# Attention stages of a two-layer decoder: head stacks split over the two halves of TensorE's rows, and row scores issued in turn with transposed scores

## The chip, the cores and the metric

The kernel runs on one core of a Trainium2 chip. The metric is the time of one execution on the device in microseconds (us). Three runs of the kernel before gave 5631.46, 5637.95 and 5650.88 us; the median is 5637.95.

Names: PE is TensorE (PEld its weight loads), DVE VectorE, ACT ScalarE, POOL GpSimd, SP SyncE, which issues nearly all DMAs here. An "S" in the text on the change means a matmul of row scores, "K" one of transposed scores, "sel" the one that adds the shift.

## The reference, cut to what matters

There are 64 batches of 128 tokens with 128 features, and a context of 77 tokens. Six sublayers follow each other, each with a residual and a layer norm behind it: a bidirectional selective scan with a feed-forward part, a gated and masked cross attention, a block of self attention and a mixture of experts, a self attention with normed queries and keys, a cross attention, and a quantized feed-forward part. The four attentions have 16 heads of 8 features. The plain one:

```python
q = _split_heads(query @ wq + wq_b, H)      # (B, H, 128, 8)
k = _split_heads(key_in @ wk + wk_b, H)     # (B, H, 128 or 77, 8)
v = _split_heads(value @ wv + wv_b, H)
logits = jnp.einsum('bhqd,bhkd->bhqk', q, k) / jnp.sqrt(8)
attn = jax.nn.softmax(logits, axis=-1)
out = jnp.einsum('bhqk,bhkd->bhqd', attn, v)
return out @ wo + wo_b
```

In the gated one a mask is added to the logits and `attn` is multiplied by a given array. All arithmetic is float32; the scores must have nearly that precision.

## The kernel before, in words

`build` (L2630 on) runs seven stages one after the other: the scan; the gated cross attention (tag `x0`, tiles named `x_...` in the trace); the self attention in front of the experts (`f0`, tiles `f_...`); the experts; the self attention of layer 1 (`a1`, tiles `a_...`); the cross attention of layer 1 (`x1`, tiles `x_...` again); the quantized part. Four of them are the function `attention` (L70). The text calls these x0, f, a and x1. From 2611 us x0 is running, from 3285 f, from 4255 a, from 4889 x1.

**Stacks.** Queries and keys are split into three bfloat16 parts each (high, middle, low) by DVE (L637, L642) and POOL (L824, L831). SP writes the parts to DRAM (`save_parts`, L237) and reads them back as stacks (`fill_stack`, L249): `Qs` and `Ks` have, for each head, 48 rows: six pairs of parts times 8 features, so that one bfloat16 matmul with 48 rows of contraction gives the scores of a head. The other 80 of the 128 partitions are zero (memsets L577 and L807), and the matmuls read all 128. A stack holds one group of four batches side by side in its columns, and there are two (parity of the group).

**Steps and chunks.** Work goes in steps, one batch each, of four chunks; a chunk is four heads. A group has 16 chunks. `turn` is two groups, and `Fori` repeats it. All engines run through the same sequence of steps and chunks and are tied by semaphores only. In the stages f, a and x1, which have no gate, chunk c of step b holds on PE:

- `scores` (L342): four matmuls, queries by keys, into one of two banks. DVE takes the maximum over the keys (`maximum`, L669), negated.
- `shifted` (L360), of batch b-1 (chunk c-1; the last chunk of it comes with chunk 0 of the next step): transposed scores, keys by queries, four times a matmul of `Ks` and `Qs` and one of `sel` with the turned maxima `nmT`, which adds the negated maximum. ACT takes the exponential into `pT` (L512).
- `values` (L380), of batch b-2: four float32 matmuls, each into its own 32 columns of the array.
- in chunk 0 `turn_max` (L353), the transpose of the split maxima of batch b-1, into the bank that the output projection uses too; DVE copies it to `nmT` (`maxima_rows`, L697) in its chunk 0.
- in chunk 1 `turn_out` (L395), in chunk 3 `turn_back` (L403) of batch b-3, and `out` (L407), the output projection of batch b-4, in chunk 3 (chunk 2 in cross attentions), which waits (L411) until `nmT` of batch b-1 is copied. A bias row with one row of contraction follows it (L414), except in a, which has no bias.
- `prep` (L309), the projections of a coming group, in the slots that `slot` (L95 to L101) gives.

In the gated stage x0 the exponential is taken on rows, and PE turns the weights instead (`turn_weights`, L372); there are no shifted scores.

DVE has in chunk 3 also `split_maxima` (L686, four small operations) and `add_residual` (L719), in chunk 2 `weighted` (L707), in chunk 1 `norm` (L738). SP's queue (`turn`, L271) is in order: load x, save parts, store, load gate, fill the stack, load the residual.

Of the kernel before, what the change touches and what calls it, by code (L numbers as in the profile page):

```python
# [13 lines left out]
P = 128  # L14
# [55 lines left out]
def attention(nc, const, banks, tag, x_in, x_out, wq, wk, wv, wo, scale, bq=None, bk=None, bv=None, bo=None,  # L70
# [15 lines left out]
    TAIL = 6  # L86
# [8 lines left out]
    if rms:  # L95
        slot = {"x": -8, "qt": -7, "kt": -6, "qn": -3, "kn": -2, "v": 3}
        later = {"v": 1, "high": 0, "middle": 1, "squares": 0, "root": 1, "norm": 2}
    elif ln is not None:
        slot, later = {"x": -5, "q": -4, "k": -3, "v": 3}, {"v": 3, "high": 1, "middle": 2}
    else:  # L100
        slot, later = {"x": -7, "q": -5, "c": -4, "k": -3, "v": 3}, {"v": 3, "high": 1, "middle": 2}  # L101
# [12 lines left out]
    with ExitStack() as st:  # L114
# [6 lines left out]
        dram_q = nc.dram_tensor(f"{tag}_q_parts", (2, PARTS, P, GT), BF16, kind="Internal").ap()  # L121
        dram_k = nc.dram_tensor(f"{tag}_k_parts", (2, sum(K_TIMES), P, kt), BF16, kind="Internal").ap()
# [22 lines left out]
        Qs = sb("Qs", [P, 2, H, GT], BF16)  # L145
        Ks = sb("Ks", [P, 2, H, kt], BF16)
# [18 lines left out]
        s_w = sem("weights"); s_setup = sem("setup"); s_zero = sem("zeroed"); s_xp = sem("x_loaded"); s_xr = [sem(f"residual_loaded{l}", 16) for l in range(2)]  # L165
# [3 lines left out]
        s_ps = sem("parts_stored", 16 * (PARTS + 1)); s_stk = [sem(f"stack_loaded{l}", 16 * (PARTS + 1)) for l in range(2)]  # L169
# [15 lines left out]
        NZ = 2 + (gate is None) + (sk < P)  # L185
# [6 lines left out]
        def columns(t, half, u, lo, n):  # L192

            c = 2 * half + u
            return t[:, 4 * c:4 * c + 4, u * VC + lo:u * VC + lo + n]

# [5 lines left out]
        def _(sp):  # L202
# [34 lines left out]
            def save_parts(g, par):  # L237
# [4 lines left out]
                save(dram_q[par], qp[:, 0])  # L242
                sp.wait_ge(s_lo.sem, s_lo.at(g, 2))
                at = 0
                for part, times in enumerate(K_TIMES):
                    save(dram_k[par, at:at + times], qp[:, 1, part:part + 1, 0:kt].to_broadcast([P, times, kt]))
                    at += times

            def fill_stack(g, par):  # L249
                def fill(stack_rows, parts):  # L250
                    sp.dma_start(stack_rows.rearrange("p h t -> p (h t)"),
                                 parts.rearrange("a (d h) t -> (a d) (h t)", d=DH)).then_inc(s_stk[par].sem, 16)
                sp.wait_ge(s_ps.sem, s_ps.at(g + 1))
                sp.wait_ge(s_use.sem, s_use.at((g - 1) * GB))
# [16 lines left out]
            def turn(i, first=False, last=False):  # L271
                for l in range(2):
# [3 lines left out]
                    if not (last and l):  # L276
                        save_parts(g + 1, 1 - l)
# [2437 lines left out]
```

## Time and profile before

The profiled execution took 5632.96 us, its span (first to last instruction) is 5630.9 us.

| engine | busy us of the span | share | instructions |
|---|---|---|---|
| PE | 4125.1 | 73% | 29561 |
| PE weight loads | 2373.7 | 42% | 29564 |
| DVE | 4485.0 | 80% | 8773 |
| ACT | 2780.7 | 49% | 6405 |
| POOL | 3082.7 | 55% | 3374 |

The busy time of PE counts matmuls whose ends are modelled, and matmuls that follow each other overlap; what a matmul costs in a stream is the distance of the starts. In the rows below "[0.20 <-DVE x]" is idle time of the engine ahead of the instruction and what ended it. The mean granted clock of TensorE was 0.856 of full speed over the span; it has two levels, 1.2 and 2.4 GHz. DMA moved 420.49 MB, at a mean of 75 GB/s.

### The profile page before, as it was taken

How to read it: one execution, taken by the hardware profiler on the slowest of the kernel's cores; microseconds unless marked ns; L12 is line 12 of the kernel's file. 1: busy time of each engine (PE TensorE's matmuls, PEld its weight loads, DVE VectorE, ACT ScalarE, POOL GpSimd, SP SyncE). 2: the span in 40 equal slices, each digit the busy share in tenths (PEclk: the TensorE clock that was granted, in tenths of full speed). 3: DMA queues.
4: the chain of work that ended last, by engine and by line, in shares of the span. 5: the costliest groups of instructions: out<-in, count | busy, mean ns of one | idle time of the engine just before them, and what ended most of it. 6: DMA issues, size and time to landing. Idle time of an engine off the chain costs nothing. (4 is left out here: it accounts for less than half of the span.)

```text
span 5630.9 us, 104474 instructions
## 1 busy us (share of the span) xinstructions
PE 4125.1 (73%) x29561; PEld 2373.7 (42%) x29564; DVE 4485.0 (80%) x8773; ACT 2780.7 (49%) x6405; POOL 3082.7 (55%) x3374
## 2 busy tenths in 40 slices
PE   5777777777777778775878858896374887699943
PEld 2333333333323233332555536665363665466621
DVE  5999999999999999995888867775145777666678
ACT  4555555455545555453666633444464444344434
POOL 6877777777777777874555532223543222323202
PEclk8989989989899989987888779996696888899965
DMA  2110111111110111112545436664124555466511
GB/s 81 64 65 34 66 66 66 51 50 66 66 59 39 66 66 66 55 44 53 92 79 93 74 73 109 111 108 144 53 82 95 96 96 91 78 117 109 99 38 30
DMA packets 319765, 420.49 MB, mean 75 GB/s; under 512 B 39955, under 2 KB 301286, under 8 KB 308710
## 3 DMA queue, kind: packets, MB, share of 16 engines
q1 hardware_dynamic: 315110, 408.16, 31.0%
q0 software_dynamic: 4352, 8.95, 0.4%
q8 instruction: 110, 1.80, 0.1%
q14 instruction: 193, 1.58, 0.1%
HBM read 307.46 MB, written 109.58 MB: 74 GB/s over the span
## 5 line engine op out<-in xcount | busy, mean ns | idle before, releaser
L2177 POOL TENSOR_TENSOR m_h<-m_dtu,m_Bb 128x512 f32<-128x512 f32 x1024 | 1584.2, 1578 | 240.8 <-PE bank L1812 234.9
L1812 PE MATMUL bank<-m_h,ident 128*128 128x512 f32 x2048 | 1211.8, 684 | 504.1 <-DVE m_h L2076 491.2
L1812 PEld LDWEIGHTS bank<-m_h,ident 128*128 128x128 f32 x2048 | 365.3, 207 | 1168.6 <-DVE m_h L2076 1011.0
L2070 DVE TENSOR_TENSOR_SCAN m_h<-m_dA,m_h 128x512 f32<-128x512 f32 x512 | 746.7, 1458 | 6.3 <-DVE m_sz L2003 5.9
L2076 DVE TENSOR_TENSOR m_h<-m_h,bank 128x512 f32<-128x512 f32 x1024 | 671.4, 656 | 4.9 <-DVE m_h L2070 3.7
L2070 DVE TENSOR_TENSOR_SCAN m_h<-bank,m_h 128x512 f32<-128x512 f32 x512 | 620.1, 1211 | 27.8 <-DVE m_sz L2003 11.8
L1959 ACT ACTIVATE bank<-m_dt,m_A 128x512 f32<-128x512 f32 x512 | 352.4, 688 | 494.0 <-DVE m_h L2070 436.0
L1959 ACT ACTIVATE m_dA<-m_dt,m_A 128x512 f32<-128x512 f32 x512 | 367.1, 717 | 430.4 <-DVE m_h L2070 426.6
L519 ACT ACTIVATE x_sm<-x_sm,x_nm 128x77 f32<-128x77 f32 x1024 | 353.5, 348 | 115.1 <-DVE x_nm L682 114.6
L859 POOL TENSOR_TENSOR x_sm<-x_sm,x_gp 128x308 f32<-128x308 f32 x256 | 219.3, 858 | 153.5 <-ACT x_sm L519 150.3
L377 PE MATMUL bank<-ident,x_sm 128*77 128x128 f32 x1024 | 197.7, 325 | 112.6 <-DVE x_pT L705 99.2
L684 DVE TENSOR_REDUCE f_nm<-bank 128x4 f32<-128x512 f32 x256 | 175.8, 688 | 116.0 <-PE bank L349 115.3
L874 POOL TENSOR_TENSOR x_var<-x_var,half_pow 128x1 f32<-128x1 f32 x128 | 69.7, 544 | 354.5 <-DVE x_var L736 354.5
L1756 PE MATMUL bank<-m_xTp,m_wck 128*128 128x512 f32 x512 | 253.8, 599 | 12.7 <-ACT m_xTp L1874 12.7
L512 ACT ACTIVATE f_pT<-bank 128x512 f32<-128x512 f32 x256 | 153.0, 598 | 220.3 <-PE bank L369 219.0
L512 ACT ACTIVATE x_pT<-bank 77x512 f32<-77x512 f32 x256 | 151.9, 593 | 214.6 <-PE bank L369 212.4
L512 ACT ACTIVATE a_pT<-bank 128x512 f32<-128x512 f32 x256 | 153.0, 598 | 206.7 <-PE bank L369 205.6
L391 PE MATMUL bank<-x_pT,x_vB 128*32 128x128 f32 x4096 | 234.2, 304 | 11.0 <-ACT x_ou L528 10.8
L684 DVE TENSOR_REDUCE x_nm<-bank 128x4 f32<-128x308 f32 x256 | 121.7, 476 | 128.3 <-PE bank L349 126.7
L874 POOL TENSOR_TENSOR a_var<-a_var,half_pow 128x1 f32<-128x1 f32 x64 | 34.7, 542 | 335.5 <-DVE a_var L736 335.5
L684 DVE TENSOR_REDUCE a_nm<-bank 128x4 f32<-128x512 f32 x256 | 175.1, 685 | 48.7 <-PE bank L349 46.7
L1805 PE MATMUL bank<-m_Cs,m_selC 80*128 80x512 bf16 x512 | 207.5, 405 | 0.0
(424 smaller groups left out, 10613.5 us busy)
## 6 DMA issues: line engine op xcount, KB each, us to landing
m_Bb<-m_B SPq DMA_DIRECT2D x32, 4096.0 KB, 12.0
x_Ks<-x_k_parts SPq DMA_DIRECT2D x32, 462.0 KB
x_q_parts<-x_qp SPq DMA_DIRECT2D x32, 384.0 KB, 3.8
x_Qs<-x_q_parts SPq DMA_DIRECT2D x32, 384.0 KB
f_Ks<-f_k_parts SPq DMA_DIRECT2D x16, 768.0 KB
a_Ks<-a_k_parts SPq DMA_DIRECT2D x16, 768.0 KB
x_xp<-x_stage SPq DMA_DIRECT2D x32, 256.0 KB
x_Qs<-x_q_parts SPq DMA_DIRECT2D x32, 256.0 KB
```

The source lines that it names most:

```text
L391: ins = pe.matmul(bankO[j * VT:(j + 1) * VT, half * S:(half + 1) * S], vB[:, lb % 2, 4 * c + j, :], pT[:, lb % 2, 4 * c + j, :], start=(c ...
L512: act.activation(pT[0:sk, p, 4 * c:4 * c + 4, :].rearrange("p h t -> p (h t)"), src, ACT.Exp).then_inc(s_e.sem, 1)
L519: ins = act.activation(sm[:, lm % 2, h, :], sm[:, lm % 2, h, :], ACT.Exp, bias=nm[:, lm % 2, 0, h:h + 1], accum_out=den[:, lm, h:h + 1])
L684: v.tensor_reduce(nm[:, p, 0, 4 * c:4 * c + 4], src, AX.X, ALU.max, negate=True).then_inc(s_Sf.sem, 1)
L859: pool.tensor_tensor(ws, ws, gp[:, lm // GB, lm % GB, :].unsqueeze(1).to_broadcast([P, 4, S2]), ALU.mult).then_inc(s_pg.sem, 1)
L1756: ins = pe.matmul(o, wck[:, d, part, c * P:(c + 1) * P], xTp[:, :, part:part + S], start=(part == 0), stop=(part == CK - 1))
L1805: pe.matmul(banks[2 + s % 2], selC[:, s, :], Cs[:, d, :], start=True, stop=True).then_inc(s_C.sem, 1)
L1812: pe.matmul(banks[4 + c], ident[:], h[:, k % RING, :], start=(s == 0), stop=(s == NS - 1)).then_inc(s_ya.sem, 1)
L1959: act.activation(decays[k % AHEAD], dt[:, d, c, :], ACT.Exp, scale=A[:, d, c, s:s + 1]).then_inc(s_dA.sem, 1)
L2070: v.tensor_tensor_scan(h[:, k % RING, :], decays[k % AHEAD], h[:, k % RING, :], 0.0, ALU.mult, ALU.add).then_inc(s_h.sem, 1)
L2076: v.tensor_tensor(h[:, k % RING, :], h[:, k % RING, :], banks[2 + s % 2], ALU.mult).then_inc(s_hC.sem, 1)
L2177: pool.tensor_tensor(h[:, k % RING, :], dtu[:, d, c, :], Bb[:, d, s, :], ALU.mult).then_inc(s_dB.sem, 1)
```

## The change

The stacks get half as many columns. A group's first two batches lie in partitions 0 to 47 of `Qs` and `Ks`, the other two in partitions 64 to 111. Each matmul on them reads 48 partitions (`rows(q)`), no longer 128, and the memsets of `Qs`, `Ks`, `nmT` and `pT` go, as does the semaphore for them; `values` reads only the rows that are written. `nmT` and `sel` exist for both halves (three more `affine_select` in the constants). SP saves and fills by halves: four more saves and four more fills per group, the same bytes. The first half may be filled as soon as the first two batches two groups back are used, and is queued ahead of the store.

In the stages without a gate the transposed scores move from one batch to two batches behind the row scores, so they always lie in the other half, and the two are issued in turn, head by head. `turn_max` moves from chunk 0 to chunk 1, `maxima_rows` to DVE's chunk 2. Everything from `values` on comes one batch later (`LATER`), and the tail is one step longer. The V projection moves from slot 3 to 4, and its evacuation to chunk 8 of a group (in a from chunk 4, else from 6). In the gated stage the order stays; only rows, memsets and DMAs change there, and the place of the V projection.

```diff
+    LATER = 1 if gate is None else 0
+    TAIL = 6 + LATER
+    HB = GB // 2
-        slot = {"x": -8, "qt": -7, "kt": -6, "qn": -3, "kn": -2, "v": 3}
-        later = {"v": 1, "high": 0, "middle": 1, "squares": 0, "root": 1, "norm": 2}
+        slot = {"x": -8, "qt": -7, "kt": -6, "qn": -3, "kn": -2, "v": 4}
+        later = {"v": 4, "high": 0, "middle": 1, "squares": 0, "root": 1, "norm": 2}
...
-        Qs = sb("Qs", [P, 2, H, GT], BF16)
-        Ks = sb("Ks", [P, 2, H, kt], BF16)
+        Qs = sb("Qs", [P, 2, H, HB * S], BF16)
+        Ks = sb("Ks", [P, 2, H, HB * sk], BF16)
...
+        def rows(q):
+            lo = 64 * (q // HB)
+            return slice(lo, lo + ROWS)
+
+        def cols(q, n):
+            return slice(q % HB * n, (q % HB + 1) * n)
...
-            def fill_stack(g, par):
+            def fill_stack(g, par, half):
...
-                sp.wait_ge(s_ps.sem, s_ps.at(g + 1))
-                sp.wait_ge(s_use.sem, s_use.at((g - 1) * GB))
+                if half == 0:
+                    sp.wait_ge(s_ps.sem, s_ps.at(g + 1))
+                sp.wait_ge(s_use.sem, s_use.at((g - 2) * GB + (half + 1) * HB))
+                lo = 64 * half
                 at = 0
                 for parts in K_TIMES:
-                    fill(Qs[at * DH:(at + parts) * DH, par], dram_q[par, 0:parts])
+                    fill(Qs[lo + at * DH:lo + (at + parts) * DH, par], dram_q[par, half, 0:parts])
                     at += parts
-                fill(Ks[0:ROWS, par], dram_k[par])
+                fill(Ks[lo:lo + ROWS, par], dram_k[par, half])
...
+                        load_gate(g + 1, 1 - l)
+                        fill_stack(g + 1, 1 - l, 0)
                     if not first:
                         store(g - 2, l)
                     if not (last and l):
-                        load_gate(g + 1, 1 - l)
-                        fill_stack(g + 1, 1 - l)
+                        fill_stack(g + 1, 1 - l, 1)
...
-            def scores(i, lb, c):
+            def scores(i, lb, c, now, then):
                 b, l, q = 8 * i + lb, lb // GB, lb % GB
...
+                tb = (lb - 2) % 8
+                tl, tq = tb // GB, tb % GB
+                if now:
+                    if c == 0 and q % HB == 0:
+                        stacked = s_stk[l][q // HB]
+                        pe.wait_ge(stacked.sem, stacked.at(i + 1))
+                    pe.wait_ge(s_Sf.sem, s_Sf.at(b, c + 1 - 2))
+                if then:
+                    pe.wait_ge(s_nmT.sem, s_nmT.at(b - 1))
+                    pe.wait_ge(s_e.sem, s_e.at(b - 2, c + 1 - 2))
                 for h in range(4):
                     hh = 4 * c + h
...
+                    if now:
+                        ins = pe.matmul(bankS[c % 2][:, h * sk:(h + 1) * sk], Qs[rows(q), l, hh, cols(q, S)],
+                                        Ks[rows(q), l, hh, cols(q, sk)], start=True, stop=True)
+                        if h == 3:
+                            ins.then_inc(s_S.sem, 1)
+                    if then:
+                        o = bankT[c % 2][0:sk, h * S:(h + 1) * S]
+                        pe.matmul(o, Ks[rows(tq), tl, hh, cols(tq, sk)], Qs[rows(tq), tl, hh, cols(tq, S)],
+                                  start=True, stop=False)
+                        ins = pe.matmul(o, sel[rows(tq), hh, 0:sk], nmT[rows(tq), tb % 2, :], start=False, stop=True)
+                        if h == 3:
+                            ins.then_inc(s_st.sem, 1)
...
-                pe.wait_ge(s_r.sem, s_r.at(b - 3))
+                pe.wait_ge(s_r.sem, s_r.at(b - 4))
...
-                    pe.wait_ge(s_nmT.sem, s_nmT.at(min(b + 4, B) if isinstance(b, int) else b + 4))
+                    pe.wait_ge(s_nmT.sem, s_nmT.at(min(b + 5, B) if isinstance(b, int) else b + 5))
...
-                if live(0):
-                    scores(i, lb, c)
+                scores(i, lb, c, live(0), gate is None and live(2))
...
-                elif c == 0:
-                    if live(2):
-                        shifted(b - 2, (lb - 2) % 8, 3)
-                    if live(1):
-                        turn_max(b - 1, (lb - 1) % 8)
-                elif live(1):
-                    shifted(b - 1, (lb - 1) % 8, c - 1)
-                if live(2):
-                    values(b - 2, (lb - 2) % 8, c)
...
+                elif c == 1 and live(1):
+                    turn_max(b - 1, (lb - 1) % 8)
+                n = 2 + LATER
+                if live(n):
+                    values(b - n, (lb - n) % 8, c)
...
-            dve.memset(Ks[:], 0.0).then_inc(s_zero.sem, 1)
-            if gate is None:
-                dve.memset(nmT[:], 0.0).then_inc(s_zero.sem, 1)
-            if sk < P:
-                dve.memset(pT[:], 0.0).then_inc(s_zero.sem, 1)
...
-                if c == 0 and live(1) and gate is None:
+                if c == 2 and live(1) and gate is None:
                     maxima_rows(v, ch, b - 1, (lb - 1) % 8)
```

## Rows read from the trace of the kernel before

**Rows 1.** stretches x0, f, a, x1: length; PE, PEld, DVE, ACT, POOL; clock; DMA
```profile
2690.00:3240.00 550.00, 445.66 (x4218) 301.08 (x4216) 476.63 (x1136) 374.30 (x1945) 306.44 (x550) 0.81 0.48 84
3400.00:3780.00 380.00, 338.67 (x4303) 241.55 (x4301) 275.10 (x798) 154.61 (x317) 102.57 (x245) 0.95 0.62 109
4330.00:4800.00 470.00, 379.35 (x4794) 287.49 (x4794) 343.25 (x934) 226.84 (x427) 117.22 (x304) 0.87 0.54 96
4950.00:5330.00 380.00, 355.30 (x5057) 258.90 (x5056) 255.01 (x934) 179.88 (x378) 115.84 (x322) 1.00 0.62 109
```

**Rows 2.** groups, DVE, same stretches: count | busy us, mean ns | idle, releasers
```profile
L679 DVE TENSOR_TENSOR x_sm<-bank,x_neg 128x308 f32<-128x308 f32 x222 | 104.6, 471 | 51.5 <-PE bank L349 50.4
...
L684 DVE TENSOR_REDUCE f_nm<-bank 128x4 f32<-128x512 f32 x187 | 128.6, 687 | 79.2 <-PE bank L349 78.8 <-issue 0.2
...
L684 DVE TENSOR_REDUCE a_nm<-bank 128x4 f32<-128x512 f32 x204 | 139.8, 685 | 37.4 <-PE bank L349 35.6
...
L684 DVE TENSOR_REDUCE x_nm<-bank 128x4 f32<-128x308 f32 x218 | 103.8, 476 | 99.6 <-PE bank L349 98.2
```

**Rows 3.** instructions in order of time, f, one chunk: start us, us, engine
```profile
3574.99 0.39 PE L349 MATMUL bank<-f_Ks,f_Qs 128*128 128x128 bf16 x4
...
3575.22 0.22 PE L367 MATMUL bank<-f_Qs,f_Ks 128*128 128x128 bf16 x1
...
3575.61 0.22 PE L369 MATMUL bank<-f_nmT,sel 128*128 128x128 bf16 x1
...
3575.76 0.43 PE L391 MATMUL bank<-f_pT,f_vB 128*32 128x128 f32 x8
...
3576.11 0.40 PE L349 MATMUL bank<-f_Ks,f_Qs 128*128 128x128 bf16 x4
```

**Rows 4.** in order of time, x1: projection, bias row, row scores, shifted scores
```profile
5154.27 0.49 PE L412 MATMUL bank<-x_w,x_oT 128*128 128x128 f32 x2
...
5154.69 0.48 PE L414 MATMUL bank<-x_bor,ones_row 1*128 1x128 f32 x2
...
5155.10 0.32 PE L349 MATMUL bank<-x_Ks,x_Qs 128*128 128x77 bf16 x4
...
5155.26 0.22 PE L367 MATMUL bank<-x_Qs,x_Ks 128*77 128x128 bf16 x1
```

**Rows 5.** in order of time, a: projection without bias, transpose
```profile
4515.76 0.49 PE L412 MATMUL bank<-a_w,a_oT 128*128 128x128 f32 x2
...
4516.08 0.27 PE L405 MATMUL bank<-ident,a_on 128*128 128x128 f32 x1
```

**Rows 6.** instruction groups, PE, stretches of f, a, a, x1
```profile
L357 PE MATMUL bank<-identb,f_nmp 128*48 128x128 bf16 x47 | 11.2, 239 | 13.1 <-DVE f_xr L725 13.0
...
L357 PE MATMUL bank<-identb,a_nmp 128*48 128x128 bf16 x51 | 11.9, 233 | 35.4 <-DVE a_r L729 33.0 <-DVE a_nmp L695 2.4
...
L367 PE MATMUL bank<-a_Qs,a_Ks 128*128 128x128 bf16 x808 | 127.8, 238 | 16.3 <-DVE a_nmT L700 16.3
...
L367 PE MATMUL bank<-x_Qs,x_Ks 128*77 128x128 bf16 x872 | 122.5, 221 | 20.3 <-DVE x_nmT L700 20.3
```

**Rows 7.** instruction group, DVE, x1: the copy of the maxima rows
```profile
L700 DVE COPY x_nmT<-bank 48x128 bf16<-48x128 bf16 x54 | 11.1, 206 | 0.0
```

**Rows 8.** in order of time, stage starts: f, f, f, f, x1, x1
```profile
3286.47 13.75 POOL L807 MEMSET f_Qs<- 128x16384 bf16 x1 [0.15 <-POOL f_vB L799]
...
3295.07 5.17 DVE L598 TENSOR_SCALAR f_lvar<-f_lst 128x4 f32<-128x4 f32 x1
...
3321.19 0.30 SPq L251 DMA_DIRECT2D f_Ks<-f_k_parts  x1
...
3336.08 1.01 PE L349 MATMUL bank<-f_Ks,f_Qs 128*128 128x128 bf16 x8 [8.18 <-issue]
...
4902.12 2.55 DVE L637 CAST x_qp<-x_qf 128x512 bf16<-128x512 f32 x1 [3.30 <-ACT x_qf L476]
...
4914.09 0.43 DVE L637 CAST x_qp<-x_qf 128x512 bf16<-128x512 f32 x1 [4.82 <-ACT x_qf L476]
```

More of the change, by code:

```diff
@@ L163, in attention @@
         lvar = sb("lvar", [P, 2, GB]) if ln is not None else None
-        s_w = sem("weights"); s_setup = sem("setup"); s_zero = sem("zeroed"); s_xp = sem("x_loaded"); s_xr = [sem(f"residual_loaded{l}", 16) for l in range(2)]
+        s_w = sem("weights"); s_setup = sem("setup"); s_xp = sem("x_loaded"); s_xr = [sem(f"residual_loaded{l}", 16) for l in range(2)]
         s_xpfree = sem("x_used"); s_pb = sem("proj_written", NU); s_pf = sem("proj_evacuated", NU)
@@ L168, in attention @@
         s_mid = sem("mid_ready", 2); s_lo = sem("lo_ready", 2)
-        s_ps = sem("parts_stored", 16 * (PARTS + 1)); s_stk = [sem(f"stack_loaded{l}", 16 * (PARTS + 1)) for l in range(2)]
+        s_ps = sem("parts_stored", 32 * (PARTS + 1)); s_stk = [[sem(f"stack_loaded{l}{half}", 16 * (PARTS + 1)) for half in range(2)] for l in range(2)]
         s_ln = sem("front_var", 1); s_lp = sem("front_pow", 1); s_xn = sem("front_norm", 1)
@@ L287, in _ @@
             save_parts(0, 0)
-            sp.wait_ge(s_zero.sem, NZ)
-            fill_stack(0, 0)
+            for half in range(2):
+                fill_stack(0, 0, half)
             turn(0, first=True)
@@ L358, in turn_max @@
                              identb[:]).then_inc(s_T.sem, 1)
-            def shifted(b, lb, c):
-                l, q = lb // GB, lb % GB
-                pe.wait_ge(s_nmT.sem, s_nmT.at(b + 1))
-                pe.wait_ge(s_e.sem, s_e.at(b, c + 1 - 2))
-                for h in range(4):
-                    hh = 4 * c + h
-                    o = bankT[c % 2][0:sk, h * S:(h + 1) * S]
-                    pe.matmul(o, Ks[:, l, hh, q * sk:(q + 1) * sk], Qs[:, l, hh, q * S:(q + 1) * S],
-                              start=True, stop=False)
-                    ins = pe.matmul(o, sel[:, hh, 0:sk], nmT[:, lb % 2, :], start=False, stop=True)
-                ins.then_inc(s_st.sem, 1)
             def turn_weights(b, lb, c):
@@ L455, in _ @@
                         prep(u, g, g)
-            pe.wait_ge(s_zero.sem, NZ)
             turn(0, first=True)
@@ L806, in _ @@
             pool.nop().then_inc(s_setup.sem, 1)
-            pool.memset(Qs[:], 0.0).then_inc(s_zero.sem, 1)
             def front(g):
@@ L2622, in _ @@
                                pattern=[[-1, P]], channel_multiplier=1).then_inc(s, 1)
-            for part in range(3):
-                pool.affine_select(out=sel[:], in_=sel[:], compare_op=ALU.not_equal, fill=1.0, base=-part * H,
+            for n, lo in enumerate((0, H, 2 * H, 64, 64 + H, 64 + 2 * H)):
+                pool.affine_select(out=sel[:], in_=sel[:], compare_op=ALU.not_equal, fill=1.0, base=-lo,
                                    pattern=[[-1, H], [0, P]], channel_multiplier=1).then_inc(s, 1)
-                pool.wait_ge(s, 8 + part)
+                pool.wait_ge(s, 8 + n)
     return {"ident": ident, "identb": identb, "ones_row": ones_row, "sel": sel, "half_pow": half_pow}
```

97 lines of the change are left out of this document (47 added, 50 removed).

## The prediction, made before the change was run

> **What bounds the kernel now.** I read the page first, then cut the span into stages with the view of stretches, then took the groups of instructions of DVE and PE in those stages, and last the instructions in order of time. The page's slices show the scan stage up to 2605 us (POOL and DVE full, PE behind them), which the change does not touch, then four attention stages. In the three without a gate PE is busy 89%, 81% and 93% of the time, DVE 72%, 73% and 67%; in the gated one DVE has 87% and PE 81% [rows 1]. The maxima per stage give the pace: 187 chunks in 380 us, 204 in 470, 218 in 380 and 222 in 550, so a group of 16 chunks (four batches) takes 32.5 us in the front attention (f), 36.9 in the layer-1 attention (a), 27.9 in the layer-1 cross attention (x1) and 39.6 in the gated one (x0). In the same rows DVE stands idle for PE's scores 78.8, 35.6 and 98.2 us [rows 2]. So f, a and x1 are bounded by PE's own stream, with some waits of PE for DVE in between; x0 is a loop in which DVE has the larger part. DMA has a mean share of at most 0.62 [rows 1], and the stacks are needed half a group after they are asked for.
>
> **What a chunk costs on PE.** At the 2.4 GHz level the row scores of f (4 matmuls) take 0.23 us from their start to the first shifted score, the 8 shifted ones follow at (3575.61-3575.22)/7 = 0.056 us, the first values matmul comes 0.15 us after the last of them, and the values take 0.35 us [rows 3]. So a chunk is 12 matmuls at their streaming rate, 0.67 us, and 0.45 us for the values and the way into them. With 77 columns the four row scores of x1 take 0.16 us at most, so a pair of load and matmul can go at 0.04 us or less [rows 4].
>
> **Row scores beside shifted scores.** The new order is S, K, sel, S, K, sel..., with S in one half of the rows and K and sel in the other. If a matmul of the other half can start beside the one in flight, the 8 of the shifted half set the length (8 x 0.055 = 0.44) and the four S hide, but for one start. That removes 0.20 of 0.23 us per chunk in f and a, 3.2 us per group, and 0.12 of 0.16, 1.9 us per group, in x1. Twelve pairs in 0.44 us are 0.037 us each, near what [rows 4] shows possible. No row shows two row halves at work together; the ends are 0 and 0.23 (f, a) or 0.16 (x1) per chunk. I take nearly the whole, because the values, four heads in four strips of 32 columns, do run beside each other: 8 in 0.35 us, which also holds a way in and out [rows 3].
> The Trainium skill, page "TensorE: Matmul & The Clock Gate", section "Part 3: Packing small matmuls — row/col tiling", says that matmuls in different row groups run at the same time, and that four of them gave 3.07 times the rate, not 4. By that share, 0.77, f and a would save 0.15 us a chunk and not 0.20, and the whole sum below would be some 32 us smaller. No row here shows it either way.
>
> **Changes of the tile shape.** A matmul with the bias row (one row of K) behind one of 128 rows costs more than its streaming: the output projection to the bias row is 0.42 us in x1, bias row to scores 0.41 [rows 4], while the same projection in a, followed by a 128-row transpose, gives way after 0.32 us [rows 5]. So a change of row shape costs 0.10 us. Before, the scores had the same 128 x 128 shape as transposes and projections; now they have 64 rows, and each way from a 128-row instruction to scores is such a change. The values and the transpose of the maxima (48 columns) already were changes on both sides. Per group: f has the output transposes and the turned-back output in each batch (8) and two projections alone in a chunk (2): 10, so 0.95 us. a: 8 and 4, 1.15 us. x1: 8 and 2, 0.95 us (the bias row at chunk 2 was one already). x0: 10 of these and one per chunk from scores to the turned weights, 26, 2.5 us of PE time. Ends: 0, if 64 against 128 rows is no change of shape, and 0.15 each, the largest way seen into another shape [rows 3].
> The Trainium skill, "TensorEngine Tiling (Array Packing)", section "Key Properties", states that changing the mode, not just the tile, drains the engine. The trace agrees where it can be seen (0.42 against 0.32 us). Without this cost the sum would be some 58 us better.
>
> **Waits that go and come.** The maxima are transposed one chunk later and needed a batch later. PE waited before that transpose 13.1 us in f (11.7 groups) and 35.4 in a (12.75 groups), and for the maxima rows 16.3 in a and 20.3 in x1 (13.6 groups) [rows 6]. That is 1.1, 4.05 and 1.5 us per group. These are moments in which DVE is behind; PE may run only two score banks ahead of it, so part comes back as a wait for a free bank. I take half in f (0.55) and a (2.0), 1.2 in x1; ends 0 and all.
> New: the output projection must wait until the maxima rows of the batch before have left their shared bank, and DVE now copies them in chunk 2, not 0. In f and a the projection stands in chunk 3, one chunk behind, and is covered. In x1 it stands in chunk 2 itself: from the start of the fused scores, 0.33 us to the last S, 0.22 for it to end [rows 6], 0.04, then DVE's maximum 0.476 [rows 2] and the copy 0.206 [rows 7], with steps 1.38 us in all; PE is there after 0.55 + 0.35 = 0.90. So 0.48 us per batch, 1.9 per group, with the scores of chunk 3 queued behind. Ends: 0 if PE is late anyway, 1 us a batch if DVE is.
> In a the V projection is now evacuated in DVE's chunk 8, the very chunk in which PE wants the bank for the next x: a maximum of 0.685 [rows 2] and a copy of as many columns from the same kind of bank, so as long, 0.22 us for S to end and some 0.2 of steps, against 0.11 + 0.45 us that PE has left, make 1.2 us per group. In f and x1 x comes later and has cover.
> x0: PE's 2.5 us per group are partly spent while it waits for DVE anyway. DVE waits for scores in 50.4 of 550 us, 9% [rows 2]. I take a quarter, 0.6 us; ends 0 and 2.5.
>
> **DMAs.** SP issues 8 instead of 4 saves and 8 instead of 4 stack loads per group, same bytes; the issue of one fill takes 0.30 us [rows 8], so some 3 us more in a queue that waits for most of a 28 to 40 us period. The first half is asked for as soon as the parts are stored, the second up to three chunks later than now, and needed two batches later. The store behind the first half has its work done later by a batch too. Nothing; if the cover failed, a late stack would cost PE microseconds per group.
>
> **Starts and ends.** The zeroing of the stacks goes. In f DVE's last step for the variance, 4 numbers a row, takes 5.17 us and ends with POOL's memset of 13.75 us at 3300.2; some 5.0 us go. In x1 DVE's first cast takes 2.55 us beside the memset and the next one 0.43, so 2.1 us go [rows 8]. In each stage the first scores wait for the whole stack: 14.9 us from its last issue in f [rows 8]. Half a stack should save up to 7.4 us, less 2 us of added issues and some latency; I take 4 us in each of four stages (ends 0 and 7). One more batch step in the tail of three stages, four values groups and transposes at 0.35 us each, costs 2 us each. Together -5.0-2.1-16+6 = -17 us.
>
> **Sum**, 16 groups a stage: f (-3.2+0.95-0.55) x 16 = -45; a (-3.2+1.15-2.0+1.2) x 16 = -46; x1 (-1.9+0.95-1.2+1.9) x 16 = -4; x0 +10; starts and ends -17. In all -102 us. The profiled execution took 5632.96 us (span 5630.9, 2 us around it), 5 us under the median 5637.95; so 5531 for such an execution, 5536 for the median, 1.8% faster.
>
> **Rivals.**
> 1. The halves do not overlap (S is streamed in its own time, or loads hold it up). Then f is +0.4, a +0.35, x1 +1.65 us a group, and with x0 and the starts the sum is +6+6+26+10-17 = +31: 5669 us, slower. For it: the loads of x1's 77-column stacks and 24 instructions in 0.44 us, faster than any row shows. Against: the strips of the values. With g us saved per chunk in f and a and 0.6 g in x1, the sum is 31-666 g; it decides below g = 0.047 us. Chance 0.12.
> 2. The granted clock falls. f has 0.95 and x1 1.00, a 0.87, with PE busy 89, 93 and 81% [rows 1]. If a shorter, more interrupted stream brings f and x1 to a's 0.87, PE-bound time grows: f's 16 x 29.7 = 475 us by (0.95/0.87-1), 43 us, and x1's 16 x 27.7 = 443 by (1.00/0.87-1), 66 us, and the sum is +7: 5645. Against: in f PE's idle share per group stays near a tenth. Chance 0.10.
> 3. DVE becomes the bound. Its heaviest chunks, 2 and 3, now hold the copy of the maxima rows too, and a has DVE busy 27 us of 36.9. Then about half of f's and a's gain stays: -57, 5581 us. Chance 0.15.
> 4. The waits go entirely and the shape changes cost nothing: f (-3.5-1.1) x 16 = -74, a (-3.5-4.05+1.2) x 16 = -102, x1 (-1.9-1.5) x 16 = -54, x0 0, starts -17: -247, 5391. A case halfway there, 5460, is the likely form. Chance 0.18.
>
> **How the numbers follow.** My forecast has 0.45 and its own range is 5490 to 5580. Two tenths left out, the range runs from the halfway case to between rivals 2 and 1: 5440 to 5655. A change under 0.3% (17 us) can't be told from none. Faster: 0.45+0.18+0.15 less a little, 0.77; rival 2 is split, same 0.09; slower 0.14.
>
> **What would show it.** After: shifted scores at 0.055 us with an S starting inside each pair, and no separate 0.23 us; PE's busy time per group down by 2 to 3 us in f and a; bias-row-like steps of 0.10 us ahead of scores; in x1 a PE wait for the maxima rows at the output projection; no wait at the transpose of the maxima; f's first pow right behind its variance. The prediction is wrong if fused chunks take over 0.60 us, if f's or x1's clock falls below 0.9, or if PE waits for a free score bank by over 2 us a group.

## The result, and the profile after

The changed kernel took 6124.69 us (median of 4 runs, 6102.91 to 6146.84) against 5638.97 for the kernel before in the same series: a ratio of 1.086 [1.082, 1.090], 486 us slower. Forecast were 5536 us and a range of 5440 to 5655. The profiled span is 6123.8 us, the mean granted clock of TensorE 0.72 where it was 0.856.

The first view is that of stretches in the middle of the four attention stages, x0, f, a and x1, which answers to [rows 1] (columns as there: length; PE, PEld, DVE, ACT, POOL busy; granted clock; DMA share and GB/s).

```profile
2740.00:3340.00 600.00, 561.82 (x3962) 343.97 (x3960) 440.15 (x1068) 351.43 (x1828) 282.12 (x524) 0.60 0.43 73
3500.00:3980.00 480.00, 431.78 (x4575) 262.13 (x4574) 295.80 (x842) 167.22 (x336) 111.37 (x264) 0.67 0.50 91
4540.00:5040.00 500.00, 453.24 (x4655) 302.43 (x4652) 337.64 (x903) 223.42 (x414) 113.07 (x298) 0.61 0.48 88
5220.00:5780.00 560.00, 537.76 (x4658) 338.88 (x4658) 241.94 (x864) 173.26 (x351) 106.51 (x302) 0.50 0.36 69
```

The clock column tells nearly all: 0.81, 0.95, 0.87 and 1.00 have become 0.60, 0.67, 0.61 and 0.50. PE is not less busy than before: 94% of x0 against 81%, 90% of f against 89%, 91% of a against 81%, 96% of x1 against 93%. In x1 the clock stands at its lower level, 1.2 GHz, all through the stretch, with PE idle for 4% of it. DVE's busy time per maximum is what it was, so it now stands idle for PE's scores far longer (the groups answer to [rows 2]).

```profile
L690 DVE TENSOR_REDUCE f_nm<-bank 128x4 f32<-128x512 f32 x199 | 136.0, 688 | 162.9 <-PE bank L372 162.6
...
L690 DVE TENSOR_REDUCE a_nm<-bank 128x4 f32<-128x512 f32 x197 | 134.1, 686 | 71.4 <-PE bank L372 69.4
...
L690 DVE TENSOR_REDUCE x_nm<-bank 128x4 f32<-128x308 f32 x200 | 95.7, 479 | 295.5 <-PE bank L372 294.5
```

The next view is f in order of time, while the clock is at 2.4 GHz (it answers to [rows 3]): L372 are row scores, L378 and L380 shifted scores and selection, L410 the values.

```profile
3640.09 0.43 PE L410 MATMUL bank<-f_pT,f_vB 128*32 128x128 f32 x8
3640.45 0.23 PE L372 MATMUL bank<-f_Ks,f_Qs 48*128 48x128 bf16 x1
3640.45 0.23 PE L378 MATMUL bank<-f_Qs,f_Ks 48*128 48x128 bf16 x1
3640.52 0.22 PE L372 MATMUL bank<-f_Ks,f_Qs 48*128 48x128 bf16 x1
3640.52 0.22 PE L380 MATMUL bank<-f_nmT,sel 48*128 48x128 bf16 x1
...
3640.86 0.22 PE L380 MATMUL bank<-f_nmT,sel 48*128 48x128 bf16 x1
3641.00 0.43 PE L410 MATMUL bank<-f_pT,f_vB 128*32 128x128 f32 x8
...
3641.78 0.48 PE L433 MATMUL bank<-f_bor,ones_row 1*128 1x128 f32 x2
3642.19 0.33 PE L424 MATMUL bank<-ident,f_on 128*128 128x128 f32 x1
3642.45 0.23 PE L372 MATMUL bank<-f_Ks,f_Qs 48*128 48x128 bf16 x1
```

Two matmuls of different halves start in the same hundredth of a microsecond (3640.45, 3640.52), and the four row scores are hidden: the chunk takes 3641.00-3640.09 = 0.91 us, where it took 1.12 ([rows 3]). So the change does on PE just what it says, and the stage is still 98 us longer, because for much of it the clock is at its lower level. In x1 at 1.2 GHz the same fused group looks so (it answers to [rows 4]):

```profile
5400.96 0.31 PE L378 MATMUL bank<-x_Qs,x_Ks 48*77 48x128 bf16 x1
5401.07 0.31 PE L380 MATMUL bank<-x_nmT,sel 48*77 48x128 bf16 x1
5401.17 0.31 PE L378 MATMUL bank<-x_Qs,x_Ks 48*77 48x128 bf16 x1
5401.28 0.31 PE L380 MATMUL bank<-x_nmT,sel 48*77 48x128 bf16 x1
5401.64 0.66 PE L410 MATMUL bank<-x_pT,x_vB 77*32 77x128 f32 x8
```

The steps are 0.107 us where they are 0.056 at the upper level, and the way from the last selection into the values is 0.36 us where it is 0.15.

The waits of the new order stand in PE's groups of f and a (they answer to [rows 6]):

```profile
L431 PE MATMUL bank<-f_w,f_oT 128*128 128x128 f32 x100 | 32.4, 417 | 22.2 <-DVE f_nmT L706 22.2
...
L388 PE MATMUL bank<-identb,a_nmp 128*48 128x128 bf16 x49 | 13.9, 285 | 1.8 <-DVE a_r L735 1.5 <-DVE a_nmp L701 0.3
...
L334 PE MATMUL bank<-ident,a_xp 128*128 128x128 f32 x48 | 12.0, 397 | 23.0 <-DVE a_vS L657 23.0
```

The starts (they answer to [rows 8]): the first scores of f come 39.1 us after the stage's first memset, not 51.1, those of x1 32.4 us and not 38.6.

```profile
3400.15 0.95 POOL L798 MEMSET f_vB<- 128x1024 f32 x1 [3.95 <-POOLq L2684]
...
3439.23 1.03 PE L372 MATMUL bank<-f_Ks,f_Qs 48*128 48x128 bf16 x8 [1.38 <-DMA f_Ks<-f_k_parts]
```

The stage times, from the stage's first memset to the issue of its last store but one (that of the 15th of 16 groups), in us, with the granted clock over that time, for this kernel and all that follow ("rows" are the partitions that a stack matmul reads). Stage times and clocks are of the one profiled execution. A stage whose program did not change came out up to 12 us apart in two kernels (a in e2 against before, 629.8 and 617.8; x0 in e12 against after, 764.8 and 757.8), so smaller differences of a stage say nothing by themselves:

| kernel | x0 | f | a | x1 | median of runs | ratio |
|---|---|---|---|---|---|---|
| before | 658.8, 0.80 | 555.2, 0.90 | 617.8, 0.85 | 480.2, 0.95 | 5638 to 5648 | 1 |
| after | 757.8, 0.59 | 653.6, 0.63 | 657.6, 0.62 | 717.1, 0.50 | 6124.7 | 1.086 |
| e1 before, 48 rows | 701.6, 0.73 | 791.6, 0.52 | 751.3, 0.56 | 659.4, 0.62 | 6260.8 | 1.110 |
| e6 before, 64 rows | 708.4, 0.72 | 775.5, 0.54 | 763.6, 0.56 | 633.5, 0.66 | 6217.2 | 1.103 |
| e8 before, 96 rows | 674.7, 0.75 | 654.4, 0.71 | 647.2, 0.79 | 506.7, 0.88 | 5808.2 | 1.029 |
| e11 before, row scores alone 48 | 701.7, 0.73 | 630.1, 0.79 | 678.1, 0.78 | 511.5, 0.93 | 5834.0 | 1.035 |
| e2 before, values 77 rows | 681.5, 0.72 | 555.5, 0.90 | 629.8, 0.84 | 486.3, 0.93 | 5666.3 | 1.004 |
| e3 after, values 128 rows | 697.2, 0.70 | 647.6, 0.64 | 660.9, 0.60 | 682.5, 0.55 | 6034.3 | 1.071 |
| e5 after, 64 and 128 rows | 696.7, 0.70 | 628.0, 0.68 | 635.6, 0.71 | 602.7, 0.70 | 5892.5 | 1.044 |
| e12 after, scores ahead | 764.8, 0.57 | 618.5, 0.71 | 658.9, 0.61 | 713.8, 0.50 | 6102.9 | 1.083 |
| e13 new order, 48 rows, no halves | 706.6, 0.69 | 752.5, 0.58 | 787.4, 0.51 | 748.5, 0.53 | 6370.8 | 1.130 |
| e4 new order, 128 rows, no halves | 654.1, 0.80 | 577.5, 0.87 | 583.3, 0.91 | 488.6, 0.95 | 5626.4 | 0.997 |
| e10 e4, maxima rows copied earlier | 650.6, 0.81 | 566.7, 0.87 | 579.7, 0.91 | 488.8, 0.92 | 5599.2 | 0.992 |
| e7 new order in a alone | 659.0, 0.80 | 558.2, 0.89 | 587.2, 0.91 | 480.5, 0.95 | 5603.7 | 0.994 |
| e9 new order in x0, a, x1, two places moved | 648.4, 0.82 | 558.2, 0.89 | 582.2, 0.90 | 454.1, 0.95 | 5560.4 | 0.985 |

### The profile page after: what moved, and what is told of

Same layout as the page of the kernel before. It is cut to its first block and busy times, and to the rows that moved or that the text cites. A ratio compares the mean times of both kernels' runs of the same rounds, so it can differ in the third digit from the quotient of the medians.

```text
span 6123.8 us, 105163 instructions
## 1 busy us (share of the span) xinstructions
PE 4794.4 (78%) x29561; PEld 2628.5 (43%) x29564; DVE 4457.9 (73%) x8764; ACT 2795.5 (46%) x6405; POOL 3018.1 (49%) x3373
## 5 line engine op out<-in xcount | busy, mean ns | idle before, releaser
L410 PE MATMUL bank<-x_pT,x_vB 77*32 77x128 f32 x4096 | 322.4, 403 | 7.7 <-issue 5.3
L396 PE MATMUL bank<-ident,x_sm 128*77 128x128 f32 x1024 | 259.6, 400 | 42.0 <-DVE x_pT L711 27.1
L372 PE MATMUL bank<-x_Ks,x_Qs 48*128 48x77 bf16 x2048 | 225.7, 246 | 28.7 <-DMA x_Ks<-x_k_parts 13.2
L378 PE MATMUL bank<-x_Qs,x_Ks 48*77 48x128 bf16 x1024 | 246.3, 313 | 0.0
L685 DVE TENSOR_TENSOR x_sm<-bank,x_neg 128x308 f32<-128x308 f32 x256 | 121.7, 475 | 170.9 <-PE bank L372 169.3
```

Of the source, the lines that this page charges most:

```text
L378: pe.matmul(o, Ks[rows(tq), tl, hh, cols(tq, sk)], Qs[rows(tq), tl, hh, cols(tq, S)], start=True, stop=False)
L396: ins = pe.transpose(bankT[c % 2][0:sk, h * S:(h + 1) * S], sm[:, lb % 2, 4 * c + h, :], ident[:])
L410: ins = pe.matmul(bankO[j * VT:(j + 1) * VT, half * S:(half + 1) * S], vB[0:sk, lb % 2, 4 * c + j, :], pT[0:sk, lb % 2, 4 * c + j, :], sta ...
```

## The experiments

**The rows that the stack matmuls read.** Before, the stacks hold numbers in 48 rows and zeros in 80, and every matmul reads all 128. The change reads 48. e1 makes this cut alone.

```
-  pe.matmul(bankS.., Qs[:, l, hh, ..], Ks[:, l, hh, ..])
+  pe.matmul(bankS.., Qs[0:ROWS, l, hh, ..], Ks[0:ROWS, l, hh, ..])   # the shifted scores and sel, nmT too
```

> The kernel before, with its order and its stacks, only that the bfloat16 matmuls on the stacks (and sel with the turned maxima) read the 48 rows that hold data and not the 80 zero rows too. Nothing can overlap, all are in the lower half. Theory (T1): the granted clock falls because these matmuls use fewer rows of the array; then x1 is near 0.50 to 0.6 and f near 0.65 as after the change, and since no scores hide, the time is at or above that of after: 6100 to 6350 us. Rival (T2): it is the overlap or the new order that lowers the clock; then x1 stays near 1.00, f near 0.95, and the time is 5640 to 5710 us (before plus 0.10 us per change of row shape).

Measured: 6260.8 us, 1.110 [1.107, 1.114]. The order, the waits and the number of instructions are those of the kernel before, and it is slower than the changed kernel: 623 us go with the rows alone. The theory of the rows has its range met (6100 to 6350 us), and its rival, the overlap or the order (5640 to 5710 us), is refuted. The stretch of its f stage (as in [rows 1]):

```profile
3328.00:4120.00 792.00, 748.16 (x5759) 492.76 (x5760) 397.56 (x1079) 213.12 (x422) 146.75 (x346) 0.52 0.40 72
```

PE is busy 94% of it and has the clock at 0.52; before it was busy 83% of the stage, at 0.90.

**The values.** In x0 and x1 the change also cuts the values from 128 rows to 77. e2 does this in the kernel before, e3 undoes it in the changed one.

```
e2:  -  vB[:, lb % 2, ..], pT[:, lb % 2, ..]          e3:  -  vB[0:sk, ..], pT[0:sk, ..]
     +  vB[0:sk, lb % 2, ..], pT[0:sk, lb % 2, ..]         +  vB[:, ..], pT[:, ..]     # pT zeroed at the start
```

> The kernel before, only that the values matmuls of x0 and x1 read the 77 rows that are written and not 128. f and a are untouched. T1 (rows in use set the clock, whatever the tile shape): x0 and x1 fall part of the way, x0 below 0.75, x1 below 0.9, time 5680 to 5850 us. If only the tile shape of 64 rows matters, 77 rows still count as 128 and nothing changes: 5620 to 5655 us. T2: nothing changes either.

> The changed kernel, with the values matmuls of x0 and x1 reading all 128 rows again (the weights tile zeroed at the start). f and a as after. T1: x0 and x1 get part of their clock back, x1 0.55 to 0.8, time 5900 to 6080 us. If the values have no part in it: 6100 to 6150 us, x1 at 0.50.

Measured: e2 5666.3 us, 1.004 [1.003, 1.005], with 23 us more in x0 (clock 0.72 for 0.80) and 6 in x1, which is too little to be read; the total lies between the ranges of the two theories (from 5680, to 5655). e3 6034.3, 90 us less than the changed kernel, 61 of them in x0 and 35 in x1, as forecast. The same cause at a second place, and the smaller one.

**The order alone.** e4 has the new order of the steps (V's new places too) and the alternating issue, with the whole stacks of before.

```
 def rows(q):
-    return slice(64 * (q // HB), 64 * (q // HB) + ROWS)
+    return slice(0, P)              # stacks, their fills and their zeroing as before
```

> The order of the changed kernel (scores in turn with transposed scores two batches behind, everything from values on a batch later, maxima turned in chunk 1) with the stacks of before: 128 rows read, one half, whole-group loads. No overlap. T1: the clock is as before (x1 over 0.95, f over 0.93), and what is left is the new order: waits for the maxima gone, a wait at the output projection in x1; 5560 to 5650 us. T2 (the order lowers the clock): over 5900 us with x1 under 0.8.

Measured: 5626.4 us, 0.997 [0.996, 0.999], clock 0.859. With whole stacks the order does not lower the mean clock. It moves time between stages: a gains 34.5 us, f loses 22.3 and x1 8.4, which alone is too little to be read. The clock moves with it, from 0.85 to 0.91 in a and from 0.90 to 0.87 in f. The whole stage a of before, then of e4 (columns as in [rows 1]):

```profile
4254.95:4872.76 617.81, 480.38 (x5992) 364.21 (x5992) 438.07 (x1160) 285.99 (x535) 160.43 (x391) 0.85 0.52 92
```

```profile
4273.60:4856.91 583.31, 452.74 (x6006) 346.43 (x6007) 437.05 (x1161) 285.76 (x536) 160.21 (x391) 0.91 0.55 97
```

PE's busy time fell by 27.6 us and its idle time only from 137.4 to 130.6, so most of the gain in a came with the clock and not with waits that went. Why the order changes the clock of a stage is open. PE's groups with the new waits, of f and x1:

```profile
L423 PE MATMUL bank<-f_w,f_oT 128*128 128x128 f32 x90 | 23.2, 342 | 25.5 <-DVE f_nmT L704 25.5
...
L423 PE MATMUL bank<-x_w,x_oT 128*128 128x128 f32 x106 | 24.3, 311 | 20.6 <-DVE x_nmT L704 20.6
```

**How many rows.** e6 and e8 are e1 with 64 and 96 rows; e11 leaves 48 rows to the row scores only, a third of the stack matmuls.

```
e6:  Qs[0:64, ..]   e8:  Qs[0:96, ..]      # with Ks, sel and nmT
e11: Qs[0:48, ..] in scores() only; shifted() reads Ks[:], Qs[:], sel[:], nmT[:]
```

> The kernel before in its own order, the scores, shifted scores and selection reading 64 rows of the stacks instead of 128 (with 48 rows it took 6260.8 us, clock 0.73; with 128 rows 5638 us, 0.86). If the clock goes by rows in proportion, 6130 us and clock 0.76. If 64 is no better than 48, 6260 us. If a change of row shape were the cause, it would be as slow as with 48 rows too, so this one is read together with 96 rows.

> The kernel before in its own order, reading 96 rows of the stacks instead of 128. The tile shape on the engine is then that of 128 rows (no added 0.10 us way between shapes is expected), so what is left is the number of rows alone. Rows theory in proportion: a quarter of the way is 32 of 80 rows, 0.4 x 622 = 250 us, so about 5890 us at a clock of 0.81. A threshold above 96 rows: near 6200 us. A cause in the shape of the tile and not in its rows: 5638 us, unchanged.

> The kernel before in its own order; only the row scores (4 of the 12 stack matmuls of a chunk) read 48 rows, the shifted scores and the selection 128. If the mean of the rows over the stream sets the granted clock, the mean is (4 x 48 + 8 x 128) / 12 = 101 rows, near the 96 of an earlier run: front attention about 640 us and clock 0.73, total about 5790 us. If what counts is the longest stretch of full rows, or if the 4 can hide among the 8, the front attention stays at 555 to 575 us and the total at 5640 to 5690. If any 48-row run spoils it, the front attention is near 790 us.

Measured: 6217.2, 5808.2 and 5834.0 us (1.103 [1.100, 1.106], 1.029 [1.026, 1.031], 1.035 [1.032, 1.038]). In proportion to the rows e6 would have taken 6130 us and e8 5890. The f stages of e8, then of e6:

```profile
3308.00:3962.00 654.00, 574.30 (x5761) 404.90 (x5762) 390.50 (x1079) 209.71 (x422) 151.38 (x346) 0.71 0.49 87
```

```profile
3340.00:4116.00 776.00, 726.42 (x5760) 478.36 (x5761) 396.62 (x1079) 212.68 (x422) 147.15 (x346) 0.54 0.41 73
```

With 128, 96, 64 and 48 rows f has the clock at 0.90, 0.71, 0.54 and 0.52: no straight line, most of the loss is there at 64 rows, where it can't fall much further (the lower level is 0.50). A change of the tile shape is not the cause: at the upper level a chunk of e8's f takes a median 1.132 us, as in the kernel before, so it pays for no change of shape, and its clock is lower all the same. e11's mean is 101 rows. Its f has the clock at 0.79, higher than e8's 0.71 and the 0.73 forecast, so a third of the matmuls with few rows lowers the clock in part; it is not spoiled by any of them, nor saved by the other two thirds. That e11 lies near e8 in time all the same (630 against 654 us in f) is in part another cost. One chunk of its f at the upper level:

```profile
3404.94 0.39 PE L349 MATMUL bank<-f_Ks,f_Qs 48*128 48x128 bf16 x4
3405.27 0.23 PE L367 MATMUL bank<-f_Qs,f_Ks 128*128 128x128 bf16 x1
```

From the row scores to the shifted ones it takes 0.33 us where it took 0.23 ([rows 3]), the 0.10 us of a change of shape, and the whole chunk a median 1.235 us for 1.132, which is up to 26 us in a stage of 256 chunks. In x0 the two can be compared directly: that stage has no shifted scores, so e11 and e1 are the same there, and take 701.7 and 701.6 us. The rows from the 49th on hold zeros: they change no result, and still the clock goes with their being read.

**Full halves.** e5 is the changed kernel with each half reading all its 64 rows.

```
-            return slice(lo, lo + ROWS)
+            return slice(lo, lo + 64)      # stacks and nmT zeroed at the start, values read 128 rows
```

> The changed kernel, but a half's matmuls (row scores, shifted scores, selection of the maxima) read all 64 rows of their half, 48 with numbers and 16 zeroed ones, and the values read 128 rows as before. Theory A (the fewer rows a matmul reads, the lower the granted clock, and zero rows count): two halves of 64 at work together fill the engine, so the clock comes back to 0.85 or more in total, f at 0.90 and more; then the overlap shows its worth: f 0.2 us less per chunk, about 5530 us in total. Theory B (each matmul is counted alone, by its own rows): 64 of 128 is little more than 48, the clock stays at 0.75 to 0.78 and the time is 5900 to 6000 us. Theory C (not the rows but the shape changes or the order): the time stays that of the changed kernel with 128-row values, 6034 us.

Measured: 5892.5 us, 1.044 [1.041, 1.047]. Theory A is refuted: two halves of 64 rows side by side don't count as one of 128, f has the clock at 0.68 and not 0.90. Theory B comes within 8 us of the total (5900) and meets the total clock (0.78), but its ground, that each matmul is counted alone, does not fit e6, which with the same 64 rows one after the other has 0.54 in f. The order of the two differs as well, so this pair does not show it by itself; e3 and e13 below do so for 48 rows. Theory C (6034 us) is refuted.

**The halves alone.** e12 was to part them by issuing the four row scores ahead of the shifted ones.

```
                         if h == 3: ins.then_inc(s_S.sem, 1)
+                for h in range(4):
+                    hh = 4 * c + h
                     if then: ...                      # shifted scores and selection
```

> The changed kernel (halves of 48 rows, the new order) with the row scores of a chunk issued together ahead of its shifted scores, so that the two halves meet only where one group follows the other. If working side by side raised the clock as well as it shortened the stream (front attention 0.67, against 0.52 for 48 rows one after the other), the front attention goes from 653.6 to about 790 us, the layer-1 attention from 658 to 740, the cross attention from 717 up, some 6350 us in total. If the 0.67 came from the order and not from the halves, only the 0.2 to 0.3 us a chunk at the lower clock are lost: front attention 700 to 730 us, 6200 in total.

Measured: 6102.9 us, 1.083 [1.077, 1.089], not to be told from the changed kernel, and neither theory's. (f took 35 us less in the profiled execution, at 0.71 for 0.63; the four executions of this kernel lie 72 us apart, so nothing is read from that.) PE in order of time shows why (L372 row scores, L380 and L382 shifted scores and selection):

```profile
3641.70 0.23 PE L372 MATMUL bank<-f_Ks,f_Qs 48*128 48x128 bf16 x1
3641.71 0.23 PE L380 MATMUL bank<-f_Qs,f_Ks 48*128 48x128 bf16 x1
3641.77 0.22 PE L372 MATMUL bank<-f_Ks,f_Qs 48*128 48x128 bf16 x1
3641.78 0.22 PE L382 MATMUL bank<-f_nmT,sel 48*128 48x128 bf16 x1
3641.82 0.22 PE L372 MATMUL bank<-f_Ks,f_Qs 48*128 48x128 bf16 x1
3641.84 0.22 PE L380 MATMUL bank<-f_Qs,f_Ks 48*128 48x128 bf16 x1
```

The first shifted score stands behind four row scores in the program and starts 0.01 us after the first of them. So this run did not part the halves. e13 does: new order, 48 rows, all in the lower rows; e3 is the same with halves (and with the loads by halves, and without the memsets of the stacks).

```
 def rows(q):
-    return slice(0, P)              # e4
+    return slice(0, ROWS)           # e13
```

> The new order with whole stacks in one place (as in the run that took 5626 us), but reading 48 rows of them: the changed kernel with 128-row values, without its two halves. That kernel took 6034 us, with 697, 666, 661 and 682 us in the four stages. If the two halves at work together gave both a shorter chunk and part of the clock back, the front attention goes from 666 to about 800 us and the layer-1 attention from 661 to 740, 6280 us in total, clock 0.52 in the front attention. If the halves gave only their 0.2 us a chunk (at the lower clock 0.3) and the clock is that of the rows alone in this order, the front attention takes 715 us at 0.64 and the total is 6130 us.

Measured: 6370.8 us, 1.130 [1.126, 1.133], beyond the figures of both theories (6280 and 6130 us), with f's clock at 0.58, midway between theirs (0.52 and 0.64). One chunk of its f stage at the full clock, in order of time:

```profile
3701.40 0.43 PE L402 MATMUL bank<-f_pT,f_vB 128*32 128x128 f32 x8
3701.76 0.23 PE L364 MATMUL bank<-f_Ks,f_Qs 48*128 48x128 bf16 x1
3701.83 0.22 PE L370 MATMUL bank<-f_Qs,f_Ks 48*128 48x128 bf16 x1
...
3702.53 0.43 PE L402 MATMUL bank<-f_pT,f_vB 128*32 128x128 f32 x8
```

Without halves the chunk takes 1.13 us, with them 0.91. At 48 rows the halves are worth 336 us, 105 in f, 127 in a and 66 in x1, with more clock too in f and a (0.64 against 0.58, 0.60 against 0.51). At the lower level the chunk takes a median 1.55 us with halves (e3) and 1.97 without (e13), so there they save 0.42 us and not 0.22.

The 486 us now add up, step by step: order (e4 against before) -12, 128 to 48 rows (e13 against e4) +744, halves (e3 against e13) -336, values to 77 rows (after against e3) +90. The terms are not independent. In the old order the same cut of the rows costs 623 us (e1), so at 48 rows the new order is 110 us slower than the old (e13 against e1: x1 +89, a +36, f -39), though it gains 12 at 128 rows. The clock differs there too (x1 0.53 for 0.62, a 0.51 for 0.56, f 0.58 for 0.52); why is open.

**What is left of the order.** e7 has it in a alone, as a copy of the attention function for that stage; e10 moves DVE's copy of the maxima rows; e9 keeps f as before and moves the projection of x1 and the evacuation of V in a.

```
e10: -  if c == 2 and live(1) and gate is None: maxima_rows(..)
     +  if c == 1 and live(1) and gate is None: maxima_rows(..)
e9:  -  out_at = 3 if ctx is None else 2
     +  out_at = 3 if ctx is None or gate is None else 2
     -  later = {"v": 4, ..}   # rms
     +  later = {"v": 3, ..}
```

> The kernel before, with the new order of the steps (shifted scores two batches behind, maxima transposed a chunk later, values three behind) and whole 128-row stacks in the layer-1 attention alone. The order alone in all four stages gave this stage 583.3 us against 617.8 and took 22 us more in the front attention and 8 in the layer-1 cross attention. If stages add up, 5638 - 34 = 5604 us; if the gain came from a change of phase against the stage before, 5638.

> The new order in all four stages with whole 128-row stacks (5626 us), DVE's copy of the maxima rows in chunk 1 instead of 2. If PE's wait for that copy at the output projection (25.5 us in the middle of the front attention, 20.6 in the cross attention) is what the order costs there, the front attention takes 577.5 - 27 = 550 us and the cross attention 488.6 - 25 = 464, 5575 us in total. If DVE, which must then wait in chunk 1 for PE's transpose of the maxima, passes the wait on to its maxima, nothing is won: 5626 us, or more.

> The kernel before in the front attention; in the other three the new order with whole 128-row stacks, and two places moved: in the layer-1 cross attention the output projection goes from chunk 2 to chunk 3, in the layer-1 attention V is evacuated by DVE in chunk 7 and not 8. If the wait for the maxima rows at the projection (20.6 us of the stage's 380 us in the middle) was the price of the new order there, the cross attention takes 488.6 less 20 to 28, 460 to 468 us, and beats the 480.2 of before; if DVE is what sets that stage, it stays at 488. If PE's wait before the x transposes (28.7 us in 470) goes with V's place, the layer-1 attention takes 555 to 565 us and not 583 to 587; if it was late for another reason, 583. With the gated stage at 654 and the front attention at 555 the total is 5560 us in the first case of both, 5610 in the second.

Measured: e7 5603.7 us, 0.994 [0.992, 0.996], as the stages had added up. e10 5599.2, 0.992 [0.989, 0.995]: the wait at the projection is gone in both stages, yet f gains 11 us of the 27, no more than two profiles of one stage can differ, and x1 nothing. In f most of it is found at the transpose of the outputs:

```profile
L416 PE MATMUL bank<-ident,f_on 128*128 128x128 f32 x46 | 16.3, 355 | 22.1 <-DVE f_on L720 22.1
```

The kernel before had its largest wait of f at that very place:

```profile
L405 PE MATMUL bank<-ident,f_on 128*128 128x128 f32 x47 | 16.1, 342 | 26.5 <-DVE f_on L716 26.5
```

So in f PE waits some 22 to 27 us in 380 for DVE in all three kernels, at different places.

In x1 the clock was 0.92 and not 0.95; why is open. e9 5560.4 us, 0.985 [0.981, 0.988], beats both kernels. x1 went from 488.6 us to 454.1, below the 460 to 468 forecast: PE's idle time in the stage fell from 65.4 to 36.9 us, and PE has no wait at its projection (group of the middle of x1):

```profile
L423 PE MATMUL bank<-x_w,x_oT 128*128 128x128 f32 x88 | 21.5, 326 | 0.0
```

In a the second theory held: the wait before the x transposes is 20.2 us in 460 for 28.7 in 470, and the stage gains 1 to 5 us, not 20 to 30. The total met the first figure all the same, which is luck in part: a is 17 to 27 us above its forecast, x0 6 us and x1 6 to 14 below theirs. The four stages give 69 of the 73 us between the two profiled spans.

## Why the prediction was wrong

**The failed step is rival 2, the granted clock**, and with it what the sum took for granted: that a matmul with 48 rows costs what one of 128 does. The sum had no term for it. The prediction gave this rival 0.10 and a price of 109 us, f and x1 falling to a's 0.87, "if a shorter, more interrupted stream" came. The stream was not interrupted, PE was as busy as ever, and in f and x1 the clock fell to 0.67 and 0.50, which the prediction had named as a sign of being wrong (below 0.9). The cut of the rows cost 623 us in the old order (e1) and 744 in the new (e13 against e4). The cause is the rows read (e1, e6, e8, e11, e13), and the diff shows it in plain sight, `Qs[:, ...]` to `Qs[rows(q), ...]`; the prediction weighed that edit as a change of tile shape only. The Trainium skill, "TensorE: Matmul & The Clock Gate", section "Part 1: The HAM clock gate", ties the clock to how busy the engine has been; by that rule alone x1, busy 96%, would have kept it, and the measurement (0.50) decides. Its section "Why this matters for your kernels" says that a single matmul of K=32 takes as long as one of K=128. In time at the full clock the traces agree for 48 rows, which start 0.056 us apart in e13 as those of 128 rows do in the kernel before, but a stream of them loses the clock.

**Overlap**: right. Forecast were 0.20 us off a chunk in f, measured are 0.21 (after against before) and 0.22 (e13 against the changed kernel) at the full clock; rival 1 is refuted.

**Changes of the tile shape**: right where seen. In f the turned-back output to the scores took a median 0.165 us before and 0.26 after (3642.45-3642.19), the forecast 0.10. At the lower level of the clock a change costs more: the way from the output transposes to the scores took a median 0.213 us before and 0.353 after.

**Waits that go**: at the transpose of the maxima in a 1.8 us in 500 are left after, of 35.4 in 470 before ([rows 6]), but at a lower clock; e4, near the clock of before, has 14.2 left there and nothing at the shifted scores (16.3 before), so more than the half that was taken went. What the prediction left out is that PE then waits elsewhere, in e4's a in front of the values (1.2 us in 470 before):

```profile
L402 PE MATMUL bank<-a_pT,a_vB 128*32 128x128 f32 x1752 | 96.2, 293 | 20.5 <-ACT a_ou L535 20.5
```

The order is worth 34.5 us in a (e4); the forecast's terms for it, -2.0 and +1.2 a group, make 13. That more came is not to the forecast's credit: 7 us of it are idle time of PE, the rest is busy time, at a clock of 0.91 for 0.85.

**Waits that come**: x1's was right in place and near in size: 0.48 us a batch forecast, 20.6/53 = 0.39 measured in e4, and 28 us of idle time in the stage when e9 removes it. In f the prediction said "one chunk behind, and is covered": it isn't, 25.5 us in e4 and 22.2 in the changed kernel; f's wait for the turned-back output (26.5 us before), which the prediction did not read, went in exchange. V's place in a was priced at 1.2 us a group; the wait is 28.7/13 = 2.2, but when e9 takes a third of it away the stage gains 1 to 5 us, so the time is bound elsewhere.

**Starts**: right in kind, low in size in f: f's first scores came 12.0 us sooner (forecast 9), x1's 6.2 (forecast 6.1). **DVE as the bound** (rival 3) can't be judged in the changed kernel, where the clock hides it. **Waits gone and free shape changes** (rival 4) did not come: a change costs 0.10 us, and e4 has new waits for those that went.

## What to carry to other kernels

Before cutting the rows of a matmul because they are zero, look whether the granted clock of that stretch is at its higher level and PE is the bound: there the zeros kept the clock, and cutting them cost 0.90 to 0.52. Row halves do shorten a stream, but here they gave back less than half of what their few rows lost; the order alone, applied stage by stage and only where its stage got shorter, was the part worth keeping (e9, 0.985). Compare a moved wait by the idle time and the clock of the whole stage, since one that goes can come back at another place. Whenever a diff changes an operand's partitions, give the clock a rival that goes down to 1.2 GHz, whatever the busy share.

## What the runs showed of the hardware

The granted clock went with the rows that the stack matmuls read, zeros included: 0.90, 0.71, 0.54 and 0.52 in f for 128, 96, 64 and 48, at a PE busy share of 83, 88, 94 and 94%. Two halves of 64 rows side by side had 0.68 (e5), two of 48 0.64 (e3), where 48 rows one after the other in the same order had 0.58 (e13). What in the engine is counted the runs do not show.

Matmuls of the two halves start in pairs even if the program has three others of one half ahead (e12: 0.01 us after the first), so alternating the issue is not needed for the overlap. The Trainium skill, "TensorE: Matmul & The Clock Gate", section "Part 2: What happens when you issue a matmul", says that matmuls stay in program order and only weight loads are pulled ahead; the starts in this trace, a shifted score at 3641.71 ahead of the second row score at 3641.77, do not agree, as far as recorded starts can tell.
